# A recommender tower on one Trainium2 core: four units as quads instead of pairs from round 17, three more rounds added by 1 MB DMAs, the gathers split over the rounds

## The reference, cut to what matters

```python
e = jnp.stack([tbl_0[ids[:, 0]], ..., tbl_39[ids[:, 39]]], axis=1)      # (512, 40, 64)
vi, vj = e[:, i_idx, :], e[:, j_idx, :]                                 # all pairs i < j
z = jnp.einsum('bpe,bpe->bp', jnp.einsum('bpd,pde->bpe', vi, W), vj)    # (512, 780)
h = jnp.concatenate([z, dense_ctx], axis=1)
h = jnp.maximum(h @ W_top1 + b_top1, 0.0)
h = jnp.maximum(h @ W_top2 + b_top2, 0.0)
y = h @ W_top3
```

## Time and profile before

| | us |
|---|---|
| median of 3 runs | 317.13 (316.91 to 317.27) |
| the profiled execution, its own time | 317.05 |
| its span, first to last instruction | 315.2 |
| TensorE busy | 309.2 |
| VectorE busy | 256.4 |
| GpSimd busy | 196.3 |
| ScalarE busy | 115.0 |

### The profile page before, as it was taken

How to read it: one execution, slowest core, us unless ns; L and a number is a source line. 1 busy time by engine, 2 the same in 40 slices (tenths; PEclk the granted TensorE clock), 3 DMA queues, 4 the chain that set the end, 5 groups by cost and what they waited for, 6 DMA issues and landing times.

```text
span 315.2 us, 4374 instructions
## 1 busy us (share of the span) xinstructions
PE 309.2 (98%) x1684; PEld 112.8 (36%) x1684; DVE 256.4 (81%) x264; ACT 115.0 (36%) x296; POOL 196.3 (62%) x156
## 2 busy tenths in 40 slices
PE   7999999999999999999999999999999999999996
PEld 2444233332233333333233332333333333333464
DVE  4995987878989898998989999999999999960000
ACT  0203820544553966389986603057000000001032
POOL 3798777777777777777763787746665555650000
PEclk9999999999999999999999999999999999999999
DMA  6980332322322573232234698877788755440000
GB/s 151 330 273 17 67 87 62 74 79 64 92 58 65 153 295 98 59 89 66 64 89 100 141 210 163 167 185 159 159 183 178 149 117 102 100 83 8 12 0 0
DMA packets 16189, 35.86 MB, mean 114 GB/s; under 512 B 3749, under 2 KB 4777, under 8 KB 14505
## 3 DMA queue, kind: packets, MB, share of 16 engines
q0 software_dynamic: 5824, 16.79, 27.9%
q1 hardware_dynamic: 7848, 13.96, 14.8%
q10 hardware_dynamic: 2496, 4.84, 4.4%
HBM read 22.86 MB, written 0.00 MB: 73 GB/s over the span
## 4 chain that ended last, share of the span: by engine, by line
PE 85%; DVE 9%; ACT 2%; issue 2%; DMA 1%; DVEq 0%
PE y_ps L645 51%; PE z_ps L669 21%; PE y_ps L679 5%; DVE prod L538 4%; PE t_ps L679 2%; DVE prod L461 2%; PE y_ps L733 2%; PE t_ps L551 2%; ACT x L393 1%; DMA lane_rows_sb<-lane_rows 1%; DVE zT L471 1%; DVE x_quad L467 1%; DVE x L461 1%; PE y_ps L551 1%; PE t_ps L733 1%
## 5 line engine op out<-in xcount | busy, mean ns | idle before, releaser
L645 PE MATMUL y_ps<-x,w 64*128 64x512 f32 x780 | 183.2, 605 | 0.4 <-DVE prod L538 0.2
L330 POOL DMA_INDIRECT gathered<-in_tbl,ids_sb x128 | 130.8, 1022 | 43.2 <-issue 37.8
L538 DVE TENSOR_TENSOR prod<-y_ps,x 128x1024 f32<-128x1024 f32 x89 | 103.7, 1211 | 17.6 <-PE y_ps L645 15.3
L538 DVE TENSOR_TENSOR prod<-y_ps,x_quad 128x1024 f32<-128x1024 f32 x96 | 110.4, 1213 | 1.3 <-issue 0.6
L645 PEld LDWEIGHTS y_ps<-x,w 64*128 64x128 f32 x780 | 70.0, 186 | 112.2 <-issue 81.2
L393 ACT COPY x<-x_fold 32x128 f32<-32x128 f32 x208 | 61.5, 295 | 64.7 <-DVE x_fold L506 60.2
L355 POOL TENSOR_TENSOR prod<-prod 128x2048 f32<-128x2048 f32 x12 | 54.5, 4538 | 33.1 <-DVE prod L538 33.1
L669 PE MATMUL z_ps<-prod,select 128*32 128x512 f32 x588 | 73.4, 600 | 0.5 <-ACT zT L422 0.5
L669 PEld LDWEIGHTS z_ps<-prod,select 128*32 128x32 f32 x588 | 14.3, 108 | 52.6 <-issue 39.1
L422 ACT COPY zT<-z_ps 128x512 f32<-128x512 f32 x6 | 3.5, 585 | 66.9 <-PE z_ps L669 66.8
L416 ACT COPY x_mix<-x 64x512 f32<-64x512 f32 x40 | 24.7, 617 | 0.7
(11 more groups left out here) (47 smaller groups left out, 82.2 us busy)
## 6 DMA issues: line engine op xcount, KB each, us to landing
w<-w_rows SPq DMA_DIRECT2D x48, 256.0 KB, 3.0
prod<-prod POOLq DMA_DIRECT2D x12, 1024.0 KB, 7.7
gathered<-in_tbl,ids_sb POOLq DMA_INDIRECT x128, 2.5
w<-w_rows ACTq DMA_DIRECT2D x1, 1792.0 KB
prod<-in_tbl ACTq DMA_DIRECT2D x6, 256.0 KB, 6.3
prod<-hot_ids SPq DMA_DIRECT2D x4, 256.0 KB, 6.4
prod<-in_tbl ACTq DMA_DIRECT2D x4, 128.0 KB, 3.0
w<-w_rows ACTq DMA_DIRECT2D x1, 512.0 KB
```

Of the source, the lines that this page charges most:

```text
L330: nc.gpsimd.indirect_dma_start(gathered[:, slot, c, s * DIM:(s + 1) * DIM], None, tables[f][:, :], bass.IndirectOffsetOnAxis(ap=ids_sb[:, ...
L538: nc.vector.tensor_tensor(prod[:, d % PROD_SLOTS, :, :], y_ps[:, d % DUO_SLOTS, :, :], factor, ALU.mult).then_inc(prod_ready, 1)
L645: last = nc.tensor.matmul(y_ps[:, d % DUO_SLOTS, half, :], w[rows, r % W_SLOTS, d % ROUND, :], x[rows, units[half], :], start=True, stop=True)
```

## The change

Units 12 and 13 become a quad, so PAIRED is 12 and there are four quads. Their rounds 17 to 22 are low and high duos; one pair duo of units 9 and 11 moves from round 16 to round 23. Rounds 17, 19 and 21 join those that are added by a 1 MB DMA (rounds 18, 20 and 22 are not added). The two steps of layer 1 move from rounds 25 and 26 to rounds 18 and 19. Units 6 and 7 are folded by VectorE and no longer transposed by TensorE, and the later folds move: those of units 8 to 12 three or four duos forward, those of units 15 to 19 back by 2 to 25 duos. 88 gathers are issued in a row; the other 40 follow the DMAs of rounds 17, 19, 21, 24, 26, 28, 30, 32 and 34. On ScalarE the eight copies of each half of a unit stand at that half's own duo.

```diff
-LAYER1_AT = [25, 26]
+LAYER1_AT = [18, 19]
...
-PAIRED = 14
+PAIRED = 12
...
-FOLD_AT = {5: (4, 7), 8: (25, 29), 9: (33, 36), 10: (40, 43), 11: (47, 51), 12: (54, 58), 13: (62, 65), 14: (69, 73),
-           15: (76, 80), 16: (84, 88), 17: (91, 95), 18: (100, 104), 19: (116, 132)}
-
-GATHERED_FIRST = 120
-GATHERS_BEHIND = {24: 2, 26: 2, 28: 2, 30: 2}
-ADDED_BY_DMA = [24, 26, 28, 30, 32, 34, 36, 38, 40, 42, 44, 46]
+FOLD_AT = {5: (4, 7), 6: (8, 12), 7: (16, 19), 8: (22, 26), 9: (29, 32), 10: (36, 40), 11: (43, 47), 12: (50, 54), 13: (58, 63),
+           14: (67, 73), 15: (78, 86), 16: (93, 97), 17: (102, 108), 18: (116, 129), 19: (138, 146)}
+
+GATHERED_FIRST = 88
+GATHERS_BEHIND = {17: 4, 19: 6, 21: 10, 24: 4, 26: 4, 28: 3, 30: 3, 32: 3, 34: 3}
+ADDED_BY_DMA = [17, 19, 21, 24, 26, 28, 30, 32, 34, 36, 38, 40, 42, 44, 46]
...
-            pairs += [("pair", k, u) for k in range(u - u % 2)]
+            own = [("pair", k, u) for k in range(u - u % 2)]
+            later = own[-1:] if u == PAIRED - 1 else []
+            pairs += own[:len(own) - len(later)]
             if u % 4 == 3:
                 pairs += self.mixed(u)
+            pairs += later
...
-                else:
-                    for e in range(ROWS // QUAD):
-                        if e % 2 == 0:
-                            act.wait_ge(unit_folded, 2 * list(FOLD_AT).index(u) + e // 2 + 1)
-                        for b in range(ROWS // QUAD):
...
+            def save_half(u, s):
+                act.wait_ge(unit_folded, 2 * list(FOLD_AT).index(u) + s + 1)
+                for e in (2 * s, 2 * s + 1):
+                    for b in range(ROWS // QUAD):
...
+                        if u in FOLD_AT:
+                            for s in range(2):
+                                if FOLD_AT[u][s] == d:
+                                    save_half(u, s)
+                        elif plan.transposed_at(u) == d:
                             save_x(u)
```

More of the change, by code:

```diff
@@ L385, in save_x @@
                     nc.scalar.copy(x[:, u, :], bank[:, :]).then_inc(x_ready, 1)
-                else:
-                    for e in range(ROWS // QUAD):
-                        if e % 2 == 0:
-                            act.wait_ge(unit_folded, 2 * list(FOLD_AT).index(u) + e // 2 + 1)
-                        for b in range(ROWS // QUAD):
-                            to = x[e * QUAD:(e + 1) * QUAD, u, :].rearrange("e (c b) -> e c b", c=CHUNKS)
-                            last = nc.scalar.copy(to[:, :, b * QUAD:(b + 1) * QUAD],
-                                                  x_fold[b * QUAD:(b + 1) * QUAD, u % 2, :, e * QUAD:(e + 1) * QUAD])
+            def save_half(u, s):
+                act.wait_ge(unit_folded, 2 * list(FOLD_AT).index(u) + s + 1)
+                for e in (2 * s, 2 * s + 1):
+                    for b in range(ROWS // QUAD):
+                        to = x[e * QUAD:(e + 1) * QUAD, u, :].rearrange("e (c b) -> e c b", c=CHUNKS)
+                        last = nc.scalar.copy(to[:, :, b * QUAD:(b + 1) * QUAD],
+                                              x_fold[b * QUAD:(b + 1) * QUAD, u % 2, :, e * QUAD:(e + 1) * QUAD])
+                if s == 1:
                     last.then_inc(x_ready, 1)
-                if u >= PAIRED:
+                if s == 1 and u >= PAIRED:
                     act.wait_ge(x_ready, u + 1)
@@ L426, in _ @@
                     for u in range(UNITS):
-                        if plan.transposed_at(u) == d:
+                        if u in FOLD_AT:
[3 more added lines that the diff above has]
+                        elif plan.transposed_at(u) == d:
                             save_x(u)
-                            if u % 4 == 3:
-                                save_mixture(u - 3)
+                        if u % 4 == 3 and d == (FOLD_AT[u][1] if u in FOLD_AT else plan.transposed_at(u)):
+                            save_mixture(u - 3)
                 if r == 12:
```

## The result

The kernel after takes 339.64 us (median of 4 runs, 337.59 to 340.16), the kernel before in the same comparison 317.19: a ratio of 1.0695, 95% interval 1.0676 to 1.0714. The forecast was 335.5 with a range of 329 to 344. The profiled execution of after is its fastest run: 337.59 us, span 335.8.

A forecast was written before the change was run, and what follows sets the result against it. TensorE's own work bounds the kernel before; in rounds 17 to 36 the add, gather, fold chain takes over. 317.05 - 1.6 + 0.5 + 1.0 + 18.5 = 335.5 us, range 329 to 344.

The forecast's parts named there:

- The step on which all hung: Rounds 17 to 36: gathers behind a 1 MB add land only after it, the add's 8.0 us and about 0.5 each.
- The first rival: Gathers behind an add land 2.5 us after their own issue, waits nearly vanish, 315.7 us; chance 0.05.
- The fit that the prediction weighed: Skill's DMA estimate, 2.0 us plus bytes at 436 KB per us: 4.4 us per 1 MB add; set aside for measured 7.8 to 8.0.
- Transposes, -1.6: Units 6 and 7 folded by VectorE: eight TensorE transposes go, 0.79 us saved for each unit.
- Rounds 7 to 9, +0.5: The old 1.35 us loss goes, but TensorE waits 1.8 or 1.9 at duo 32 on GpSimd's pace; net +0.5 us.
- Unit 13, +1.0: Fold at duo 58 waits 0 to 3.3 us for gathers held up by the w1 and w2 load; taken as +1.0.
- T17 to T36, +18.5: End of VectorE's round 17 to end of round 36: add, gather, fold chain takes 113.7 us against 95.2.
- T24: End of VectorE's round 24, put 44.0 us after the end of round 17.
- 8.0 and 0.5 a gather: Rounds 17 to 36: landing time of an add in us, plus the time for each gather behind it.
- The clock rival: Granted clock falls to half in the waits, 3.6 us each: 357 us, or 342 in every third; chance 0.09, centre 345.
- The named signs: Idle before six folds, TensorE idle 15 to 20 us before line 652, rounds 38 to 47 at 4.63, eight transposes fewer.
- the six folds: Folds of duos 78, 86, 93, 129, 138 and 146, each to wait 2 to 5 us for the gathers' DMA.

The follow-up runs named there:

- e2: Kernel after without the adds by DMA of rounds 17 to 34 (TensorE sums instead), gathers issued at the same places; 323.60 us, ratio 1.0222 to before.
- e5: Kernel after with half the bytes (512 KB) in each add by DMA up to round 34, those sums incomplete; 321.18 us, ratio 1.0124 to before.
- e7: e1 with the load of w1 and w2 issued at round 15 instead of round 12; 313.58 us, ratio 0.9862 to before.
- e4: Kernel after with its last three folds later, at duos 134, 141 and 150 instead of 129, 138 and 146; 326.36 us, ratio 1.0291 to before.
- e1: Kernel after with the gathers for the folds of rounds 19 to 36 moved behind an earlier add or ahead of the first; 315.99 us, ratio 0.9978 to before.
- e3: Kernel after without the adds of rounds 17, 19 and 21, gathers and folds of units 15 to 19 as before; 319.43 us, ratio 1.0066 to before.
- e8: e1 with the folds of units 9 to 13 one to three duos later and w1 loaded at round 15; 312.20 us, ratio 0.9835 to before.

## Why the prediction was right, step by step

**What bounds.** The step on which all hung, that no gather lands before the add in front of it, held: behind the add of round 17 only packets of 8 KB move until 138, and the last of its four gathers lands at 140.94; e2 and e5 show that with the add gone or halved the waits go or shrink. The first rival (gathers land beside the add, 315.7) falls by the same runs. The Trainium skill (DMA: Bandwidth & Descriptors, section Two DMAs through the same engine are not ordered) says that within one queue of one DMA engine descriptors start in order; the trace agrees, in that none of the gathers' packets moves in the add's stretch from 132.4 to 138. The fit that the prediction weighed, 4.4 us for 1 MB, does not agree: these adds took 7.7 to 9.6.

**Transposes, -1.6.** As forecast. TensorE's timeline of after has rounds 7, 8, 9 and 10 at

```profile
67.12 3.70 PE L652 MATMUL y_ps<-x,w 64*128 64x512 f32 x16
...
72.61 2.85 PE L652 MATMUL y_ps<-x,w 64*128 64x512 f32 x12
75.94 1.13 PE L652 MATMUL y_ps<-x,w 64*128 64x512 f32 x4 [0.49 <-DVE prod L545]
...
78.85 2.85 PE L652 MATMUL y_ps<-x,w 64*128 64x512 f32 x12
...
84.78 3.70 PE L652 MATMUL y_ps<-x,w 64*128 64x512 f32 x16
```

Round 7 of before starts at 66.86 + 1.85 = 68.71: 1.6 earlier now.

**Rounds 7 to 9, +0.5.** Measured -0.2. From the start of round 7 to that of round 10 it takes 17.7 us (67.12 to 84.78), before 17.9 (68.71 to 86.57, the sum of the earlier trace rows at 84.65 and its 1.92). The forecast put one wait of 1.9 at duo 32; there were two of 1.0, at duos 32 and 36. What sets their size is open: in e7 the same two folds waited 1.1 and 2.2, though its row of gathers starts within 0.2 us of that of after (the gather at 28.16 in after is at 28.32).

**Unit 13, +1.0.** Too small. The wait was foreseen as 0 to 3.3 and is 2.7 us; from the start of round 10 to that of round 17 it takes 40.5 us (84.8 to 125.3) against 38.4 before, so it cost 2.1. VectorE came 0.5 us before it was due and the gathers landed at 113.0, inside the forecast's 110.5 to 114. The choice of +1.0, "nearer to the low end since the loads move too", failed: the load was issued at 103.8, three us earlier than before, and the gathers still met it. e7, which moves only that load, has no wait there.

**T17 to T36, +18.5.** 114.6 against a forecast of 113.7, so +19.4. T24 is 44.6 behind T17 (forecast 44.0), the add of round 30 starts 31.9 behind T24 (forecast 32.9). GpSimd's timeline, line 355, has the adds; idle time before them is the round's product, or nothing once GpSimd itself is late:

```profile
131.47 0.97 POOL L355 DMA_DIRECT2D prod<-prod  x1 [8.58 <-DVE prod L545]
...
143.95 0.96 POOL L355 DMA_DIRECT2D prod<-prod  x1 [6.37 <-DVE prod L545]
...
187.53 1.02 POOL L355 DMA_DIRECT2D prod<-prod  x1
...
198.22 1.02 POOL L355 DMA_DIRECT2D prod<-prod  x1
...
207.65 0.99 POOL L355 DMA_DIRECT2D prod<-prod  x1
```

From the add's issue to the fold (forecast 8.0 and 0.5 a gather, in brackets): duo 78 9.5 (10.0), 86 10.9 (10.0), 93 9.2 (9.0), 108 10.4 (10.0), 116 9.7 (10.0), 129 8.6 (8.5), 138 9.0 (9.0), 146 10.7 (9.5). Right on the mean to 0.25 us; those of duos 86 and 146 were 0.9 and 1.2 longer. For duo 146 the add itself took 9.6; for duo 86 it took 8.1, and the gathers behind it were late.

**The clock rival.** It came, small. In after the granted clock fell three times, to half (1.2 of 2.4 GHz), behind the three longest of the eight waits (folds of duos 86, 129 and 146, 3.7 to 4.4 us). Windows of after: stretch, its length, busy time by engine, granted clock, DMA share, GB/s; the second stretch is longer than its fall, and four duos in it take 5.40 us (from 217.95) instead of 3.70.

```profile
156.70:160.10 3.40, 3.40 (x10) 1.32 (x10) 3.11 (x3) 3.30 (x8) 1.95 (x2) 0.50 0.29 60
214.00:222.00 8.00, 4.93 (x20) 1.96 (x14) 5.29 (x6) 4.82 (x12) 4.41 (x3) 0.79 0.39 105
245.40:248.80 3.40, 3.40 (x10) 1.13 (x8) 3.40 (x4) 3.30 (x7) 0.97 (x1) 0.50 0.38 77
```

The length of the wait alone does not decide: in e4 the fold of duo 86 waits as long (4.39 us, in after 4.42), the clock stays full from 150 to 168, and the one fall comes behind the fold of duo 93.

The last fall of after costs 1.1: T36 to the start of round 38 takes 4.5 us (245.75 to 250.28), before 3.4, and in e5, which waits for the same fold at full clock, 3.3. The first costs nothing that can be seen: from the fold of duo 86 to that of duo 93 it is 12.2 us in after and 12.25 in e4. The fold of duo 93 waits for its gathers in either case, 2.7 us in after and 3.9 in e4: the slow matmuls were paid out of that wait. The prediction's 3.6 us for a fall was too much for either. The half speed that it reckoned with is what these stretches show, but the earlier trace rows, from which it took it, do not: there the granted clock is in its top tenth, in the first slice of the earlier trace rows as in all others. The Trainium skill (TensorE: Matmul & The Clock Gate, section HAM oscillation — how this bites in real kernels) says that the cost comes back with every wait; the trace has falls behind three of eight waits, and a cost that shows behind one.

**The sum.** By the end of VectorE's round 17 the forecast has 0.1 us gained (-1.6 + 0.5 + 1.0), and after has 0.05 lost (131.16, before 131.11), so 0.15 over. That is luck: the rounds up to 10 came 0.7 better than forecast and unit 13 came 1.1 worse, which leaves 0.4 in TensorE's rounds and 0.15 on VectorE. The chain adds 0.9 and the clock 1.1, together 2.15, where 2.1 are to be explained against the profiled 337.59. The median is 2.05 above the profiled run, and no trace shows where; mean granted clocks of the other runs are 0.980 to 0.985 as here, so it is not mainly the clock. That the gathers' row got going later in them, as between e1 and e3, would fit, as would longer waits at duos 32 and 36; both are only argued.

**Signs.** The named signs came: waits at the six folds (1.6 to 4.4 us rather than 2 to 5, those of duos 78 and 138 under 2), TensorE idle 16.5 us before line 652 because of VectorE, rounds 38 to 47 at 4.63, and eight transposes fewer.

## What to carry to other kernels

In this kernel the gathers that a fold waited for behind a 1 MB add on the same queue were there 8.6 to 10.9 us after the add's issue, and 2.5 us after their own where no add stood in front (e2). Where a trace shows the same, small transfers that a consumer needs soon belong ahead of the large one, or behind an earlier one. In a cycle such as product, add, gather, fold, product, a few positions decide whether it is off the path or is the path: the last 40 gathers, moved up, gave back 23.7 us, three folds moved back 13.3. When a change with real gains comes out slower, look for the first consumer that waits in the trace and move its producer before the change is given up.

## What was not expected of the hardware

A fall of the granted clock cost nothing that shows where the next fold waited for its gathers anyway (duo 86 to 93), and 1.1 us where no fold followed (behind duo 146). Of two waits of the same length, one had a fall behind it and one had none (duo 86 in after and in e4). A fold with four gathers behind an add came up to 10.9 us after the add's issue (duo 86), 0.9 more than 8.0 and 0.5 a gather. The first gathers run at uneven lengths. GpSimd's timeline of e3:

```profile
21.04 5.13 POOL L333 DMA_INDIRECT gathered<-in_tbl,ids_sb  x1 [0.30 <-issue]
```

The same gather in e8:

```profile
21.62 2.76 POOL L333 DMA_INDIRECT gathered<-in_tbl,ids_sb  x1 [0.30 <-issue]
```

Why is open. Before, which has no folds of units 6 and 7, does not wait for it; in e3 the fold at 42.41 does.
